# Two wide attentions: most keys and values made in the first score step, and the norm spread by transposes

## The reference

```
m, v = mean(x, -1), var(x, -1);  n = (x - m) / sqrt(v + 1e-5)
q = n @ Wq + bq;  k = ctx @ Wk + bk;  v = ctx @ Wv + bv      # 16 heads of 8
scores = q @ k.T / sqrt(8)       # layer 0: masked by a 256 x 512 mask
out = softmax(scores) @ v @ Wo + bo
x = x + out
```

## Time and profile before

| what | us |
|---|---|
| median of three runs | 1614.13 |
| the profiled execution | 1604.65 |
| its span in the profile | 1602.9 |
| first wide attention, first score to first logit | 198.01 to 219.17 |
| second wide attention, the same | 952.35 to 973.31 |

### The profile page before, as it was taken

One profiled execution on the slowest core, in us unless ns is written; L12 is line 12 of the kernel. 1 busy time (PEld: TensorE's weight loads), 2 busy tenths in 40 slices (PEclk: granted clock), 3 DMA queues, 4 the chain that ended last, 5 costly groups with the idle time before them and its releaser, 6 DMA issues. The chain is left out here.

```text
span 1602.9 us, 30499 instructions
## 1 busy us (share of the span) xinstructions
PE 1422.3 (89%) x10976; PEld 711.8 (44%) x11002; DVE 991.9 (62%) x1940; ACT 804.8 (50%) x1498; POOL 456.0 (28%) x656
## 2 busy tenths in 40 slices
PE   7988999999999999778987898889978788978887
PEld 5766634444364444346643452222335333523344
DVE  5776598887262221465557679999285666456646
ACT  4554537667533333214440045777754466446637
POOL 7122300000004565320136330000021456235621
PEclk9999999999999999889997899999986999999988
DMA  2000552111300000001000074321100531143100
GB/s 103 2 0 0 158 175 86 46 48 27 121 0 1 0 0 1 0 7 46 12 7 1 0 206 142 88 58 45 34 1 9 178 99 43 60 156 97 46 1 27
DMA packets 82394, 85.46 MB, mean 53 GB/s; under 512 B 7244, under 2 KB 67916, under 8 KB 81772
## 3 DMA queue, kind: packets, MB, share of 16 engines
q1 hardware_dynamic: 82296, 84.18, 17.1%
HBM read 51.06 MB, written 32.51 MB: 52 GB/s over the span
## 5 line engine op out<-in xcount | busy, mean ns | idle before, releaser
L1337 ACT ACTIVATE arena<-ps 128x1024 f32<-128x1024 f32 x256 | 262.1, 1024 | 109.3 <-PE ps L1244 108.7
L1229 PE MATMUL ps<-k_stack,q_stack 49*128 49x512 bf16 x512 | 190.5, 382 | 14.8 <-DVE small L1360 12.5
L1244 PE MATMUL ps<-q_stack,k_stack 51*128 51x256 bf16 x1024 | 189.4, 272 | 0.6 <-ACT arena L1337 0.4
L1357 DVE CUSTOM_DVE_ANT_0 small<-ps,mask_b 128x512 bf16<-128x512 f32 x256 | 168.0, 689 | 29.7 <-PE ps L1229 28.2
L1360 DVE TENSOR_REDUCE small<-ps 128x1 f32<-128x512 f32 x256 | 161.9, 684 | 16.0 <-PE ps L1229 14.9
L1546 DVE TENSOR_REDUCE small<-ps 128x6 f32<-128x768 f32 x128 | 122.6, 958 | 75.9 <-PE ps L1426 73.4
L1256 PE MATMUL ps<-arena,v_pad 128*32 128x256 f32 x2048 | 162.3, 391 | 1.1 <-ACT arena L1337 1.1
L1523 ACT ACTIVATE arena<-ps 128x384 f32<-128x384 f32 x256 | 118.0, 488 | 77.5 <-PE ps L1448 76.7
L1134 POOL TENSOR_SCALAR_AFFINE_SELECT arena<-arena 128x256 f32<-128x256 f32 x256 | 101.8, 406 | 85.9 <-ACT arena L1523 85.5
L2678 POOL TENSOR_TENSOR arena<-arena 128x512 f32<-128x512 f32 x64 | 79.7, 1266 | 92.5 <-ACT arena L2573 92.5
L2604 DVE TENSOR_TENSOR arena<-ps,arena 128x512 f32<-128x512 f32 x64 | 44.2, 691 | 99.7 <-PE ps L2521 98.8
(11 more groups left out here) (357 smaller groups left out, 2936.3 us busy)
## 6 DMA issues: line engine op xcount, KB each, us to landing
q_stack<-q_scratch SPq DMA_DIRECT2D x128, 96.0 KB
k_stack<-k_scratch SPq DMA_DIRECT2D x64, 192.0 KB
k_scratch<-arena SPq DMA_DIRECT2D x8, 768.0 KB, 3.9
k_stack<-k_scratch SPq DMA_DIRECT2D x64, 96.0 KB
q_scratch<-arena SPq DMA_DIRECT2D x4, 1152.0 KB, 7.1
arena<-in_ctxT SPq DMA_DIRECT2D x8, 512.0 KB, 6.4
k_scratch<-arena SPq DMA_DIRECT2D x8, 512.0 KB, 4.7
k_scratch<-arena SPq DMA_DIRECT2D x16, 256.0 KB, 4.2
```

The source lines that it names most:

```text
L1229: pe.matmul(ps[:, t, :], c.q_stack[par][64 * e:64 * e + ROW_MAX, pr, t * P:(t + 1) * P], c.k_stack[par][64 * e:64 * e + ROW_MAX, pr, :], s ...
L1244: mm = pe.matmul(ps[:, bank, (ch % 2) * S:(ch % 2 + 1) * S], c.k_stack[prv][64 * e:64 * e + ROWS, pr, ch * P:(ch + 1) * P], c.q_stack[prv] ...
L1337: act.activation(buf.probs[i % 8], ps[:, bank:bank + 2, :].rearrange("p a n -> p (a n)"), ACT.Exp, scale=scale).then_inc(g["probs"].sem, 1)
L1357: dve.tensor_tensor_reduce(buf.junk[t], ps[:, t, :], c.mask_b[:, M_X + t * SC:M_X + (t + 1) * SC], 1.0, FLOOR, op0=ALU.add, op1=ALU.max, a ...
```

## The change

In the two wide attentions, project makes only the key units 0 and 1, ordered key 0, query 0, key 1, queries 1 to 3; the remaining six units (batches 2 to 7) are made by a new class, LateKeys. Their steps lie at the end of project (positions -2 and -1) and in heads 0 to 10 of the first score step, two heads for each unit: key product, four value products, ScalarE's part 0 from PSUM, then TensorE adds the negated part 0 to the same bank (a bf16 product with a negated identity, `less_b`), ScalarE rounds what is left to part 1, TensorE subtracts that too, and ScalarE rounds the last rest to part 2. ScalarE also copies the values out. The clock-keeping products of the first score step stay only in heads 11 to 15. The bias of the values is left out of the copies, and GpSimd adds it as it pads them. SyncE waits for the late parts before it stores keys of batches 2 and above. In all norms the spread is made by transposes. One VectorE operation at the start of the kernel makes `less_b`.

```diff
@@ begin, vector
+            dve.tensor_scalar(c.less_b[:, :], c.consts[:, C_IDENT:C_IDENT + P], -1.0, None, ALU.mult)
@@ norm_spread
-        mm = c_matmul(pe, out[:, j * P:(j + 1) * P], rstd[:, j:j + 1].to_broadcast([P, P]), c.ident[:, :])
+        mm = pe.transpose(out[:, j * P:(j + 1) * P], rstd[:, j:j + 1].to_broadcast([P, P]), c.ident[:, :])
@@ class LateKeys
+    def keys(self, pe, v):
+        pe.wait_ge(ctx_in.sem, ctx_in.at(16))
+        if v > 1:
+            pe.wait_ge(g["late_part"].sem, g["late_part"].at(3 * (v - 1)))
+        pe.matmul(c.ps[:, self.banks(v)[0], :], self.w[:, W_K:W_K + P], self.kv_src[:, u * NT:(u + 1) * NT],
+                  start=True, stop=True, skip_group_check=True).then_inc(g["late_proj"].sem, 1)
...
+    def less(self, pe, v, a):
+        pe.wait_ge(g["late_part"].sem, g["late_part"].at(3 * v + a + 1))
+        pe.matmul(c.ps[:, self.banks(v)[0], :], c.less_b[:, :], self.part(v, a), start=False, stop=True, skip_group_check=True)\
+          .then_inc(g["late_less"].sem, 1)
+    def tensor(self, pe, at, half):
+        v = at // 2 + 1
+        if at % 2 == 0 and half == 0 and 1 <= v <= len(self.units):
+            self.less(pe, v - 1, 1)
+        if at % 2 == 0 and half == 1 and v < len(self.units):
+            self.keys(pe, v)
+        if at % 2 and half == 0 and v < len(self.units):
+            self.values(pe, v)
+        if at % 2 and half == 1 and v < len(self.units):
+            self.less(pe, v, 0)
+    def scalar(self, act, at):
+        v = at // 2 + 1
+        if at % 2 == 0 and 1 <= v <= len(self.units):
+            act.wait_ge(g["late_less"].sem, g["late_less"].at(2 * v))
+            self.keep_part(act, v - 1, 2)
+        if at % 2 == 0 and v < len(self.units):
+            act.wait_ge(g["late_proj"].sem, g["late_proj"].at(v + 1))
+            self.keep_part(act, v, 0)
+        if at % 2 and v < len(self.units):
+            act.wait_ge(g["late_value"].sem, g["late_value"].at(v + 1))
+            act.activation(self.vt[:, 4 * u:4 * u + 4, :].rearrange("p c e -> p (c e)"), c.ps[:, self.banks(v)[1], :], ACT.Identity)\
+               .then_inc(g["late_kept"].sem, 1)
+            act.wait_ge(g["late_less"].sem, g["late_less"].at(2 * v + 1))
+            self.keep_part(act, v, 1)
@@ project
+        if wide:
+            order = (("k", 0), ("q", 0), ("k", 1), ("q", 1), ("q", 2), ("q", 3))
-        for u in range(4, 4 * NKU):
-            count("k", u)
@@ project, tensor (scalar and vector alike)
         for t in TS:
-            if from_ctx:
+            if wide and t == 1:
+                tile(0)
+            if from_ctx and not (wide and t > 1):
                 unit("k", t)
...
             norm.spread(pe, t)
             if t < 3:
                 norm.variance(pe, t + 1)
-            if t:
+            if t > wide:
                 tile(t - 1)
         tile(3)
-        if from_ctx:
-            for u in range(4, 4 * NKU):
-                unit("k", u)
...
+        if wide:
+            for at in (-2, -1):
+                for half in range(2):
+                    late.tensor(pe, at, half)
@@ attend_transfers
+    def store_keys(k):
+        if made.late:
+            sp.wait_ge(g["late_part"].sem, g["late_part"].at(6 * k))
+        store_parts(c, sp, "k", nk, k, k + 1, g[f"stored_k{k}"].sem)
@@ attend_pool
+                    bv = made.late.bv.rearrange("p (h d) -> p h d", h=H).unsqueeze(1).to_broadcast([P, nch, H, DH])
+                    pool.tensor_tensor(out, rows, bv, ALU.add).then_inc(g["v_padded"].sem, 1)
@@ attend_wide, tensor
-                if not back:
+                if not back and i > 2 * len(made.late.units) - 2:
                     keep_clock(c, pe, 2)
...
                 if front:
                     score_unit(i, 0, s, par, first)
+                if not back:
+                    made.late.tensor(pe, i, 0)
...
                     score_unit(i, 1, s, par, first)
+                if not back:
+                    made.late.tensor(pe, i, 1)
@@ attend_wide, scalar
+        for at in (-2, -1):
+            made.late.scalar(act, at)
...
+                if not back:
+                    made.late.scalar(act, i)
```

More of the change, by code:

```diff
@@ L777, in project @@
     RING = (5, 6, 7, 0, 1)
+    wide = from_ctx and nk == SC
     units, used = [], []
@@ L800, in bank_of @@
         return RING[used.index((kind, n)) % 5]
+    late = None
+    if wide:
+        shared = max(n + 1 for kind, n in used if kind == "rest" and bank_of(kind, n) in (2, 3, 4, 5))
+        late = LateKeys(c, w, kv_src, kpart, vt, range(2, B), NKU, shared)
     def sync(sp):
@@ L996, in advance @@
             g.advance(gate_in=4, gate_out=4)
-    return Program(sync, tensor, scalar, vector, gpsimd, advance, len(units), nv, norm)
+        if wide:
+            late.advance()
+    return Program(sync, tensor, scalar, vector, gpsimd, advance, len(units), nv, norm, late)
 def load_stacks(c, sp, par, hf, q_at, k_at, nk, key_mask_at=None):
@@ L1126, in step @@
                     pool.wait_ge(g["summed"].sem, g["summed"].at((s - 1) * GROUPS))
-                pool.tensor_copy(c.v_pad[par][:, 0:nch, :, 0:DH],
-                                 buf.vt[:, bass.ds(s * (SC // P), nch), :].rearrange("p c (h d) -> p c h d", h=H))\
-                    .then_inc(g["v_padded"].sem, 1)
+                out = c.v_pad[par][:, 0:nch, :, 0:DH]
+                rows = buf.vt[:, bass.ds(s * (SC // P), nch), :].rearrange("p c (h d) -> p c h d", h=H)
+                if made.late:
+                    if back and not before:
+                        pool.wait_ge(g["late_kept"].sem, g["late_kept"].at(len(made.late.units)))
+                    bv = made.late.bv.rearrange("p (h d) -> p h d", h=H).unsqueeze(1).to_broadcast([P, nch, H, DH])
+                    pool.tensor_tensor(out, rows, bv, ALU.add).then_inc(g["v_padded"].sem, 1)
+                else:
+                    pool.tensor_copy(out, rows).then_inc(g["v_padded"].sem, 1)
             if back and causal:
```

50 lines of the change are left out of this document (42 added, 8 removed).

## The result

The changed kernel takes **1650.3 us** (median of 4 runs, 1637.8 to 1654.8) against 1612.7 us (1601.7 to 1616.9) for the kernel before, run in turn with it: a ratio of 1.023, 95% interval 1.019 to 1.027. The prediction was 1619.7 us, with a range to 1632. The direction was right, the size far off: some 38 us instead of 6.

A forecast was written before the change was run, and what follows sets the result against it. TensorE, busy for 89% of the span, was taken to bound the norms and wide projections. Terms of -13.8 + 0.2 + 0 + 12.8 + 6.4 = +5.6 us on 1614.1 gave 1619.7 us, range 1607 to 1632.

The forecast's parts named there:

- The transposes: In 12 norms of 4 spreads, each spread by transposes saves 0.45 us of TensorE: -13.8 us, bounds -18.0 to -8.
- Rival C: In the norms, spreads made as transposes let the clock fall: +12 us, 1631.7 us; chance 0.17.
- The wide projection: Twice: fewer key units, but later stores decide; first score at 197.9 against 198.01, nothing won or lost (-1 to +2 us each).
- The first step at full clock: First score step of both wide attentions: five rounds of 3.9 us against VectorE's 2.64, +12.8 us for both.
- Rival B: In the first score step TensorE's queue never waits for ScalarE's parts, round 3.1 us: -5.6, 1608.5 us; chance 0.12.
- The clock behind the gap: TensorE idle 6.5 us before the first score, so both score steps start at half clock: +6.4 us, 8.2 at most.
- Rival A: The clock holds over the gap before the first score: 0.8 us faster, 1613.3 us; chance 0.14.
- The start: Negated identity on VectorE ahead of the first norm: +0.2 us, between 0.1 and 2.0 if it sits out the next memset.

The follow-up runs named there:

- e1: The kernel before with only the norm's spread made by transposes: 1598.4 us, ratio 0.990.
- e8: The kernel of e7 with 48 clock-keeping products instead of 38 at the end of each wide projection: 1629.0 us, ratio 1.010 to the kernel before.
- e11: The kernel of e8 with its spreads as f32 products again instead of transposes: 1635.9 us, ratio 1.013 to the kernel before.
- e12: The kernel of e8 with 64 f32 transposes of the identity in place of its 48 clock-keeping products: 1641.1 us, ratio 1.015 to the kernel before.
- e9: The kernel of e8 with three late units made behind the wide projection in place of the 48 clock keepers (6 left): 1614.8 us, ratio 0.999 to before.
- e5: The kernel of e4 with the negated identity made behind the first norm instead of ahead of it: 1640.1 us, ratio 1.016 to the kernel before.
- e7: The kernel of e5 with a late unit's value products split around the first correction: 1634.4 us, ratio 1.015 to the kernel before.
- e4: The changed kernel with 38 clock-keeping products instead of 6 at the end of each wide projection: 1636.7 us, ratio 1.012 to the kernel before.
- e2: The kernel before with only the negated identity made ahead of the first norm and not used: 1617.2 us, ratio 1.003.
- e3: The changed kernel with its spreads as f32 products again instead of transposes: 1652.2 us, ratio 1.024 to the kernel before.
- e10: As e9 but with all five late units of the step made behind the wide projection: 1624.6 us, ratio 1.008 to the kernel before.

## Why the prediction was right, and where it was wrong

**The transposes: right, alone.** -13.8 said, -14.1 measured (e1), with the 0.44 us from spread to variance. The interval of e1 is 8 to 24 us, so the match to 0.3 us is luck in part. How much of it is left in the changed kernel isn't settled: 6.9 us by the medians of the one clean pair (e8, e11), 13.0 by their profiled executions, and next to nothing between the two executions compared above (-2.4 us outside start and wide stages). Half clock would account for the last: 28 us more of it, outside the start and the wide stages, at 0.39 to 0.5 us lost for each, is 11 to 14 us. That the transposes bring it is not shown: e1 has 20 us more of it than before, e8 7 us more than e11, each by one execution. Rival C had named this result with a mechanism that e12 speaks against, for there transposes in an unbroken row hold the clock.

**The wide projection: right.** Stores were said to come 1.8 us later in their stage; they come 2.1 and 1.9 us later (10.95 and 10.77 us behind the first scaling instead of 8.88 and 8.89). Landing took 7.8 and 8.1 us for 7.4 said, first load to score 5.3 and 5.6 for 4.9. First score +1.0 and +1.4, inside the -1 to +2. Six key and value products less gave nothing, as said.

**The first step at full clock: mechanism right, the round mis-sized.** Said 3.9 us for a round, measured 4.60. The wait was right: from the first correction to the second 1.17 us, for 1.24 said. The rest was said to issue in 2.66 us and took 3.43. I had priced a 512-column product at a quarter of an f32 key product, 0.22 us. That is what a correction takes in the gap of e9, ahead of a product with other weights (0.23 us from 196.74 to 196.97, 0.22 from 197.91 to 198.13). In the step every score of 49 rows stands between products of 128 rows, and there the starts lie 0.32 us apart, and the keys and values take 1.06 and 1.09 us instead of 0.88 and 0.90. Five rounds of 1.96 us over VectorE's 2.64 make 9.8 of the +10.1 of e5's second attention, where +6.4 was said and 9 was the upper end: **3.7 us short in each step, 7 in both.** Rival B fell with it, the queue does wait, and even without the wait (e7) a round is 4.15.

**The clock behind the gap: mechanism right, length wrong, and this is the step that failed.** An idle TensorE of over 5 us and half clock behind it came as said. But I took the length of the low stretch from the two examples of the earlier trace rows and gave 8.2 us as most for both attentions (the first, read as 3.9 us, is 3.3 by its window). It lasted 28 us, twice. The same trace of before held a longer one that I had not used, from 1197 to 1227, the slice at 6 in the earlier trace rows:

```profile
1196.00:1227.00 31.00, 23.03 (x59) 11.77 (x60) 22.33 (x41) 14.69 (x23) 6.48 (x4) 0.51 0.04 11
```

At half clock a round is 7.55 us for 4.60, so 0.39 of each us is lost: 28 x 0.39 = 11 us a step, against 3.2. **8 us short in each, 16 in both.** e4 and e8 confirm that the stop brings it: with most of the gap filled the low stretch shrinks to 4 us and the steps by 10, with all of it filled there is none. Over all traces, none of the 14 first steps without a stop ahead of the first score has a low stretch, and 10 of the 14 with a stop of 0.8 us or more have one. Rival A (the clock holds) was wrong.

**The start: wrong, and named.** +0.2 us said, with 2.0 as the upper end "if VectorE has to sit out the next memset". It can have to: the first scaling is 3.2 us later in e2 and 7.0 us later in the changed kernel, of which 1.7 us are the copies' own delay, while in e3 the first variance isn't late. What I left out was the low clock there, 17 us more of it in the first 60. The late start of the norm can't be its only source, since e7, e10 and e12 have 11 us more than before with the first variance on time. Moved behind the norm, the operation no longer delays the first variance (11.02 in e5, 11.01 in e7).

Together: 6.8 (start) + 16.3 (low clock in the steps) + 7.4 (rounds) + 2.3 (approach) + 11.4 (what the rest of the program lacks of the -13.8) is 44.2 us, and 50.0 less 5.6 is 44.4. This is for one long execution; by the medians the miss is 31 us.

**What stays open.** Why a low stretch lasts 4, 10, 20 or 28 us. The length of the stop doesn't say it: 7.80 us was followed by 10 us at half clock (e3) and 7.37 by some 30 (changed), 1.87 by 27 and 1.44 by none (e5). The share of busy TensorE in the stretch doesn't either: 92% in e3's, 96% in e5's, 100% in the 20 us of e12. It may also be why the executions of one kernel scatter, but this isn't shown: e9, with both steps at full clock, scatters over 23 us in ten runs, and e4 over 10 in four.

## What to carry to other kernels

Before you move work away from a busy engine, ask what that work was the cover of: here the key and value products had been what TensorE did while the stacks landed, and once they were gone there was a gap, a low clock and a longer step, where putting three of five units back into the gap (e9) brought the time back to that of before. It won nothing beyond: e9 is 16 us over e1, which has the transposes and no late work. Price a stop of TensorE by the longest low stretch in the trace and not by a mean, and prefer an order without a stop. Test the parts of a bundled change one by one: one of its three parts was worth 14 us (e1, 1598.4 us), and the bundle hid it.

## What was not expected of the hardware

- The granted clock stayed at 0.50 for 28 us with TensorE busy for 94 to 96% of them, and came back in 6 us of work in another execution of nearly the same step (e3). In e12 it stayed at 0.50 for 20 us with TensorE busy throughout.
- f32 transposes with nothing else held the clock at 1.00 for 7.15 us (e12).
- One small VectorE operation, started just behind the start of a GpSimd memset, took 1.90 us in one kernel and 3.61 in another, in each case to the memset's end.
- Where a product of 49 rows stands next to one of 128 rows, their starts lie about 0.1 us further apart: 0.32 us for 512 bf16 columns, where the keepers run 0.22 apart (48 in 10.5 us). Other weights alone don't do it: 0.22 to 0.23 us between the correction and the next product in e9.
